# The node stage after the first attention hands over transposed pairs four and three at a time, and sums over node types with two additions

## The chip, the cores and the metric

The kernel runs on one core of a Trainium2 chip. The metric is the device time of that core in microseconds (us). The engines have short names: PE is TensorE (PEld is its weight load), DVE is VectorE, ACT is ScalarE, POOL is GpSimd, and SP is SyncE, which issues the plain DMAs. The granted clock is the share of TensorE's full clock that the chip gave; 0.50 is its level of 1.2 GHz and 1.00 that of 2.4 GHz.

## The reference, cut to what matters

A graph network with 12,500 nodes of 64 features and 200,000 edges runs four layers, each on the normalised node features, each adding its result to `x`. The change lies in the node stage of the first layer, behind the sums over the edges:

```
k, q, v = typed_linear(x, Wk|Wq|Wv, ntype)            # first phase
alpha   = softmax of the edge scores over each dst     # edge phase
h       = segment_sum(m * alpha, dst)                  # edge phase: numerators and denominators
return typed_linear(h, Wa, ntype)                      # THIS stage: a 64x64 matrix for each of 4 node types

def typed_linear(x, W, types):
    out = 0
    for t in range(4):
        out = out + where(types == t, x @ W[t], 0.0)
    return out
...
x = x + first_layer                                    # THIS stage
h = maximum(_layernorm(x), 0.0)                        # THIS stage: the second layer's input
z = h @ Wa ; gate_proj = h @ Wg ; scores               # THIS stage: the second layer's table of node rows
```

The kernel works out `x @ W[t]` for all four types at once (256 columns), multiplies by a one-hot of the node's type and adds the four parts.

## The kernel before, in words

The phases follow each other with a barrier between: a first phase, the edge phase of the attention, a short carry phase, the node stage of this case (`attention_end_phase`), the edge phase and the node stage of the second layer, and three layers of edge sums. In all the edge phases POOL issues one indirect DMA of 128 rows after another (L864), 7820 in all.

In the node stage 12,544 padded nodes lie as 98 tiles of 128 nodes. They are worked in 7 groups (`GROUPS`) of 14 tiles (`GRP`), so a tensor of a group is 128 x 14 x 64, 896 numbers in each partition. Two tiles lie side by side, 128 features wide, and make a pair; a group has 7 pairs (`HALF`). For group i:

- POOL fetches the group's edge sums with 14 indirect DMAs (L1208); all 98 are issued at the stage's start, in order of the groups. When a group's scores are ready it writes them out with 14 more (L1214).
- DVE `take(i)` waits for the 14 fetches, divides the sums by the denominators and leaves the messages in `msg` (L1236, L1238, L1242).
- PE `out_of_group(i)` turns each pair by a transpose into a PSUM bank `ps_t` (L1324), ACT copies it to `ht` (`copy_turned`, L1288), and PE multiplies it with the four types' matrices (L1340): two products for a pair, on the upper and the lower 64 rows, into two banks `ps_o`. With y counting pairs, the transpose of pair y+1 stands ahead of the products of pair y. There are two `ps_t` banks and two `ht` buffers.
- DVE `give(i)` takes two pairs at once (`TWOS`): it multiplies PSUM with the one-hot into `sel` (L1254, twice for each of the four z), sums the four types (L1259), adds to X (L1261), normalises into H (`norm_cols`, L253 to L268; its square root is on ACT, `norm_root`, L275) and works out the scores `s2` (L1265, L1268).
- PE and ACT `rows_of_group(i)` turn the 7 pairs of H the same way, multiply them with `W1` (L1358) into `ps_r`, and ACT copies three pairs at a time (`THREES`) to `rows` (L1309), which SP stores.

The orders on the engines are written out by hand. DVE runs take(0), then for each i: take(i+1), keep_gate(i-2), give(i). ACT runs for each i: the copies of the messages of group i, `rows_of_group(i-1)`, the square root of group i. PE runs for each i: `out_of_group(i)`, `rows_of_group(i-1)`. So the square root that DVE needs in the middle of give(i) stands on ACT behind all of the rows of group i-1. `s_mm` counts finished message pairs, `s_hmm` finished rows pairs, `s_tr` transposes and `s_ht` copies.

Of the kernel before, what the change touches and what calls it, by code (L numbers as in the profile page):

```python
# [27 lines left out]
P = 128  # L28
N = 12500
E = 200000  # L30
D = 64
# [1130 lines left out]
def attention_end_phase(nc, ctx, g, agg):  # L1162
# [3 lines left out]
    s_sel, s_upd = map(sem, ("selected", "updates"))  # L1166
# [21 lines left out]
    assert len(TWOS) % 2 == 0  # L1188

    def turn_of_message(i, y):  # L1190
        return y if i == 0 else HALF + (i - 1) * 2 * HALF + y

    def turn_of_h(i, y):
        return (2 * HALF * (i + 1) if i < GROUPS - 1 else 2 * HALF * GROUPS - HALF) + y

    with ExitStack() as inner:
# [33 lines left out]
        def _(dve):  # L1230
            v = nc.vector
            def take(i):
# [7 lines left out]
                if i >= 2:  # L1240
                    dve.wait_ge(s_tr, turn_of_message(i - 2, HALF - 1) + 1)
# [4 lines left out]
            def give(i):  # L1246
                cols = slice(i * GRP, i * GRP + GRP)
                for z, ys in enumerate(TWOS):
                    dve.wait_ge(s_mm, i * HALF + ys[-1] + 1)
# [9 lines left out]
                v.tensor_reduce(upd, sel.rearrange("p t (k f) -> p t f k", k=NT), AX, ALU.add).then_inc(s_upd, 1)  # L1259
# [25 lines left out]
        def _(act):  # L1285
            def copy_turned(n):
                act.wait_ge(s_tr, n + 1)
                nc.scalar.copy(ht[n % 2], ps_t[n % 2][:, 0:P]).then_inc(s_ht, 1)  # L1288

            def messages_of_group(i):  # L1290
                for y in range(HALF):
                    if y < 2:
                        wait(act, s_hmm, (i - 1) * HALF)
                    wait(act, s_mm, i * HALF + max(y - 1, 0))
                    copy_turned(turn_of_message(i, y))

            def rows_of_group(i):
                for w, ys in enumerate(THREES):
                    for y in ys:
                        if y < 2:  # L1300
                            wait(act, s_mm, min(i + 2, GROUPS) * HALF)
                        wait(act, s_hmm, i * HALF + max(y - 1, 0))
                        copy_turned(turn_of_h(i, y))
                    act.wait_ge(s_hmm, i * HALF + ys[-1] + 1)
# [16 lines left out]
        def _(pe):  # L1321
            def turn(n, pair):
                wait(pe, s_ht, n - 1)
                nc.tensor.transpose(ps_t[n % 2][:, 0:P], pair, g.ident[:, :]).then_inc(s_tr, 1)  # L1324

            def out_of_group(i):
                pe.wait_ge(s_msg, i + 1)
                pair = lambda y: msg[i % 2][:, 2 * y:2 * y + 2, :].rearrange("p t f -> p (t f)")
                turn(turn_of_message(i, 0), pair(0))
                for y in range(HALF):  # L1330
                    n = turn_of_message(i, y)
                    if y + 1 < HALF:
                        turn(n + 1, pair(y + 1))
                    pe.wait_ge(s_ht, n + 1)
                    z, slot = y // 2, y % 2
                    if slot == 0:
                        wait(pe, s_sel, i * len(TWOS) + z - 1)
                    for b in range(2):
                        r = slice(b * D, b * D + D)
                        ins = nc.tensor.matmul(ps_o[b][z % 2][:, slot * NT * D:(slot + 1) * NT * D],  # L1340
                                               ht[n % 2][r, :], g.Wout[r, :], start=True, stop=True)
                    ins.then_inc(s_mm, 1)

            def rows_of_group(i):
                pe.wait_ge(s_n, (i + 1) * NORM_OPS)
                pair = lambda y: g.H[:, i * GRP + 2 * y:i * GRP + 2 * y + 2, :].rearrange("p t f -> p (t f)")
                turn(turn_of_h(i, 0), pair(0))
                for w, ys in enumerate(THREES):
                    for slot, y in enumerate(ys):
                        n = turn_of_h(i, y)  # L1350
                        if y + 1 < HALF:
                            turn(n + 1, pair(y + 1))
                        pe.wait_ge(s_ht, n + 1)
# [959 lines left out]
```

## Time and profile before

| | us |
|---|---|
| median of 3 runs | 13276.4 (13261.65 to 13276.62) |
| profiled execution, device time | 13250.5 |
| its span | 13248.7 |
| the node stage in it: first fetch (L1208) to the start of the last score DMA (L1214) | 2700.2 to 3022.8 |
| first work of the next phase | 3035.9 |

The stage is 323 us of 13,249, 2.4%. The profile counts an engine as busy while an instruction runs. PE's ends are modelled: its rows tell when an instruction was handed to the array and how long it should take, and who waits for its result shows when that was there. The bracket in a row of the timeline is the engine's idle time before it and what ended it; "remote" there means that the profile knows no instruction whose end fits, and "issue" that no wait is seen. The profiled execution is 26 us shorter than the median of the three runs and 11 us shorter than the shortest.

### The profile page before, as it was taken

What the parts mean: (1) busy time and instruction counts of PE and PEld (TensorE: products, weight loads), DVE (VectorE), ACT (ScalarE), POOL (GpSimd) and SP (SyncE); (2) the same over time, 40 slices, a digit from 0 to 9 for tenths busy, and PEclk for the clock granted to TensorE, in tenths of its full rate; (3) what the DMA queues carried; (4) which work ended last, traced back from release to release, by engine and by line L of the source; (5) the groups of instructions that cost most, each with busy time, mean ns of one, the idle gap of its engine ahead of it and who ended that gap; (6) DMA issues with size and microseconds to landing.
All of it is one profiled execution on the core that took longest, in us unless ns stands there. A gap on an engine that the chain in (4) does not pass through costs nothing. (4 is left out here: it accounts for less than half of the span.)

```text
span 13248.7 us, 37564 instructions
## 1 busy us (share of the span) xinstructions
PE 1392.0 (11%) x6735; PEld 1006.9 (8%) x6735; DVE 4039.7 (30%) x5465; ACT 3484.7 (26%) x4624; POOL 9102.4 (69%) x8728
## 2 busy tenths in 40 slices
PE   5200000030000000395000000200000000000000
PEld 3100000010000000273000000100000000000000
DVE  2255555544544544695111111011111101111110
ACT  2322322312222222275332222122211212221121
POOL 4677777757777776402777777577777767777776
PEclk8655555555555555697555555555555555555555
DMA  7333333313333333001222222111111111111111
GB/s 283 132 99 95 95 100 96 95 31 89 94 99 95 94 94 87 14 1 31 62 58 61 58 58 58 42 50 46 49 46 46 48 39 50 46 49 46 46 48 42
DMA packets 404824, 919.06 MB, mean 69 GB/s; under 512 B 171046, under 2 KB 195277, under 8 KB 389496
## 3 DMA queue, kind: packets, MB, share of 16 engines
q0 software_dynamic: 278944, 386.91, 13.3%
q1 hardware_dynamic: 121832, 529.42, 10.9%
q14 instruction: 176, 1.44, 0.0%
q10 hardware_dynamic: 3824, 0.50, 0.0%
q8 instruction: 48, 0.79, 0.0%
HBM read 456.45 MB, written 459.77 MB: 69 GB/s over the span
## 5 line engine op out<-in xcount | busy, mean ns | idle before, releaser
L864 POOL DMA_INDIRECT arena<-tab,src x6256 | 6544.2, 1046 | 2893.7 <-issue 2103.0
L2235 DVE TENSOR_TENSOR_SCAN arena<-cv_keep,arena 128x768 f32<-128x768 f32 (+1 forms) x476 | 752.0, 1627 | 5754.5 <-issue 4533.5
L864 POOL DMA_INDIRECT arena<-tab,spread x1564 | 1651.7, 1056 | 510.2 <-issue 510.2
L2097 ACT COPY arena<-arena 128x1472 f32<-128x1472 f32 x204 | 545.3, 2673 | 3002.8 <-DMA arena<-tab,src 3002.8
L2102 ACT COPY arena<-arena 128x1472 f32<-128x1472 f32 (+1 forms) x204 | 588.4, 2884 | 552.4 <-DVE arena L2235 463.2
L1089 PE MATMUL e_t<-ident,arena 128*68 128x128 f32 (+1 forms) x2 | 0.8, 394 | 4426.1 <-PEq L1424 2216.7
L2159 PE MATMUL cv_t<-ident,arena 128*81 128x128 f32 (+1 forms) x294 | 138.0, 469 | 2912.8 <-ACT arena L2109 1671.9
L2096 ACT COPY arena<-arena 128x368 f32<-128x368 f32 x68 | 55.3, 813 | 1351.3 <-issue 1322.7
L2173 PE MATMUL cv_t<-ident,arena 128*64 128x128 f32 (+1 forms) x3 | 1.3, 425 | 3391.4 <-ACT arena L2102 3391.4
L951 ACT ACTIVATE ae_prob<-arena 128x92 f32<-128x92 f32 x68 | 17.1, 251 | 1228.4 <-issue 942.8
L1874 DVE TENSOR_SCALAR arena<-arena 128x448 bf16<-128x448 f16 x1252 | 325.2, 329 | 43.2 <-issue 21.1
L1493 DVE TENSOR_TENSOR arena<-arena,ge_small 128x23 f32<-128x23 f32 x68 | 13.3, 195 | 1065.3 <-DMA arena<-tab,src 1065.3
L1089 PEld LDWEIGHTS e_t<-ident,arena 128*68 128x68 f32 (+1 forms) x2 | 0.3, 131 | 4426.4 <-issue 4426.4
L1757 PE MATMUL po_u<-arena,Hn 128*128 128x448 bf16 x1564 | 301.4, 355 | 289.7 <-DVE Hn L1864 289.7
L1025 DVE TENSOR_TENSOR arena<-arena,ae_prob 128x1472 f32<-128x1472 f32 x68 | 260.1, 3825 | 219.6 <-issue 215.5
L1456 ACT ACTIVATE ge_decay<-arena 128x768 f32<-128x768 f32 x68 | 56.4, 830 | 1015.0 <-issue 902.1
L992 DVE TENSOR_TENSOR_SCAN ae_work<-ae_keep,arena 128x768 f32<-128x768 f32 x136 | 240.1, 1765 | 221.8 <-remote 146.6
L1757 PE MATMUL po_u<-arena 128*128 128x448 bf16 x1564 | 298.8, 352 | 0.2 <-DVE arena L1874 0.2
L943 ACT ACTIVATE ae_work<-arena 128x768 f32<-128x768 f32 x136 | 208.4, 1533 | 300.8 <-issue 261.0
L2159 PEld LDWEIGHTS cv_t<-ident,arena 128*81 128x81 f32 (+1 forms) x294 | 53.9, 183 | 2949.7 <-ACT arena L2109 1683.0
L1034 DVE TENSOR_TENSOR_SCAN arena<-ae_work,arena 128x768 f32<-128x768 f32 x136 | 238.8, 1756 | 115.2 <-issue 101.7
L1497 DVE TENSOR_TENSOR arena<-arena,ge_small 128x1472 f32<-128x1472 f32 x68 | 258.7, 3804 | 0.2 <-issue 0.2
(369 smaller groups left out, 7017.6 us busy)
## 6 DMA issues: line engine op xcount, KB each, us to landing
rows<-arena SPq DMA_DIRECT2D x68, 1506.5 KB
arena<-tab,src POOLq DMA_INDIRECT x6256
rows3b<-arena SPq DMA_DIRECT2D x136, 736.0 KB
rows<-arena SPq DMA_DIRECT2D x68, 920.0 KB
rows<-arena SPq DMA_DIRECT2D x68, 828.0 KB
tab<-arena SPq DMA_DIRECT2D x49, 1024.0 KB
q_start<-arena SPq DMA_DIRECT2D x32, 1564.0 KB
arena<-q_start SPq DMA_DIRECT2D x68, 736.0 KB
```

Of the source, the lines that this page charges most:

```text
L864: pool.indirect_dma_start(out=rows[b][:, j, :], out_offset=None, in_=table, in_offset=bass.IndirectOffsetOnAxis(ap=idx[:, at:at + 1].bitca ...
L943: return nc.scalar.activation(works.rearrange("p (h d) j -> p h d j", h=HH), args[:, 0, :, h0:h0 + HH].rearrange("p j h -> p h j").unsquee ...
L992: v.tensor_tensor_scan(out=work[:, :], data0=keep[:, :], data1=qts[:, x * HF * C1:(x + 1) * HF * C1], initial=0.0, op0=ALU.mult, op1=ALU.a ...
L1025: v.tensor_tensor(mix[:, :, 1:C1].rearrange("p (h d) j -> p j h d", h=H), kv[:, :, D:2 * D].rearrange("p j (h d) -> p j h d", h=H), prob.u ...
L1034: ins = v.tensor_tensor_scan(out=part, data0=work[:, :], data1=part, initial=0.0, op0=ALU.mult, op1=ALU.add)
L1497: v.tensor_tensor(peak[:, :, 1:C1].rearrange("p f j -> p j f"), r[:, :, D:2 * D], pre.unsqueeze(2).to_broadcast([P, C, D]), ALU.mult).then ...
L1757: ins = nc.tensor.matmul(ps_u[:, x, 0:half], wide[c % 2][:, x * P:x * P + P, j], ring[:, n % RING, :], start=(n == 0), stop=(n == J - 1))
L1874: v.tensor_scalar(ring[:, n % RING, :], iota_hi, hi[:, n:n + 1], None, ALU.is_equal).then_inc(s_hot, 1)
L2097: nc.scalar.copy(chain[:, 0:D, 1:C1], rin[b].rearrange("p j f -> p f j")).then_inc(s_in, 1)
L2102: nc.scalar.copy(rows.rearrange("p j f -> p f j"), chain[:, :, 1:C1]).then_inc(s_copied, 1)
L2159: nc.tensor.transpose(ps_t[b][0:K_Z, 0:P], hd[b][:, 0:K_Z], g.ident[:, :]).then_inc(s_tr, 1)
L2235: ins = v.tensor_tensor_scan(out=part, data0=keep[:, 0:(f1 - f0) * C1], data1=part, initial=0.0, op0=ALU.mult, op1=ALU.add)
```

## The change

Turned pairs are handed over in batches. The messages of a group go as four pairs and three (`FOURS`), the rows as three, three and one (`THREES`): PE writes a batch of transposes side by side into one bank and signals once, ACT copies the whole bank part with one instruction into an `ht` buffer four times as wide, and PE then multiplies the batch. `s_mm` is now counted once per two pairs, and `s_hmm` once per batch. Both batches of messages are turned before the first product. On ACT the next batch of rows is copied before the products of the present one are copied out. On DVE the sum over types becomes an addition of the left 128 columns of `sel` to the right 128 (in place), and one of the left 64 to the next 64. The bytes, the products and the fetches are the same.

```diff
-        ht[b], at = view(g, at, P)
+        ht[b], at = view(g, at, 4, P)
...
+    FOURS = [range(y, min(y + 4, HALF)) for y in range(0, HALF, 4)]
...
-                v.tensor_reduce(upd, sel.rearrange("p t (k f) -> p t f k", k=NT), AX, ALU.add).then_inc(s_upd, 1)
+                v.tensor_tensor(sel[:, :, 0:2 * D], sel[:, :, 0:2 * D], sel[:, :, 2 * D:4 * D], ALU.add).then_inc(s_half, 1)
+                dve.wait_ge(s_half, i + 1)
+                v.tensor_tensor(upd, sel[:, :, 0:D], sel[:, :, D:2 * D], ALU.add).then_inc(s_upd, 1)
...
-            def copy_turned(n):
+            def copy_turned(n, count):
                 act.wait_ge(s_tr, n + 1)
-                nc.scalar.copy(ht[n % 2], ps_t[n % 2][:, 0:P]).then_inc(s_ht, 1)
+                nc.scalar.copy(ht[n % 2][:, 0:count, :].rearrange("p t f -> p (t f)"), ps_t[n % 2][:, 0:count * P])\
+                  .then_inc(s_ht, 1)
 
             def messages_of_group(i):
-                for y in range(HALF):
-                    if y < 2:
-                        wait(act, s_hmm, (i - 1) * HALF)
-                    wait(act, s_mm, i * HALF + max(y - 1, 0))
-                    copy_turned(turn_of_message(i, y))
+                for u, ys in enumerate(FOURS):
+                    wait(act, s_hmm, (i - 1) * len(THREES))
+                    wait(act, s_mm, i * len(TWOS))
+                    copy_turned(turn_of_message(i, u), len(ys))
+
+            def turned_rows(i, w):
+                if w < 2:
+                    wait(act, s_mm, min(i + 2, GROUPS) * len(TWOS))
+                wait(act, s_hmm, i * len(THREES) + max(w - 1, 0))
+                copy_turned(turn_of_h(i, w), len(THREES[w]))
...
             def out_of_group(i):
                 pe.wait_ge(s_msg, i + 1)
                 pair = lambda y: msg[i % 2][:, 2 * y:2 * y + 2, :].rearrange("p t f -> p (t f)")
-                turn(turn_of_message(i, 0), pair(0))
-                for y in range(HALF):
-                    n = turn_of_message(i, y)
-                    if y + 1 < HALF:
-                        turn(n + 1, pair(y + 1))
+                for u, ys in enumerate(FOURS):
+                    turn(turn_of_message(i, u), pair, ys)
+                for u, ys in enumerate(FOURS):
+                    n = turn_of_message(i, u)
                     pe.wait_ge(s_ht, n + 1)
```

On PE, at the start of the stage (group 0's messages; `ao_t0` and `ao_t1` are the two banks of transposes, `ao_o..` the banks of products), these rows stood before:

```order
L1324 MATMUL ao_t0<-ident,arena 128x128
L1324 MATMUL ao_t1<-ident,arena 128x128
L1340 MATMUL ao_o00<-Wout,arena 128x256
L1340 MATMUL ao_o10<-Wout,arena 128x256
L1324 MATMUL ao_t0<-ident,arena 128x128
L1340 MATMUL ao_o00<-Wout,arena 128x256
L1340 MATMUL ao_o10<-Wout,arena 128x256
L1324 MATMUL ao_t1<-ident,arena 128x128
```

And at the same place in the changed kernel:

```order
L1332 MATMUL ao_t0<-ident,arena 128x128 x4
L1332 MATMUL ao_t1<-ident,arena 128x128 x3
L1349 MATMUL ao_o00<-Wout,arena 128x256
L1349 MATMUL ao_o10<-Wout,arena 128x256
L1349 MATMUL ao_o00<-Wout,arena 128x256
L1349 MATMUL ao_o10<-Wout,arena 128x256
L1349 MATMUL ao_o01<-Wout,arena 128x256
L1349 MATMUL ao_o11<-Wout,arena 128x256
```

The seven transposes stood between the products one by one and now stand ahead of them; the number of both is unchanged.

On ACT, between two square roots in the middle of the stage (message copies, then those of the rows of the group before), these rows stood before:

```order
L275 ACTIVATE arena<-arena 128x14
L1288 COPY arena<-ao_t 128x128 x10
L1309 COPY arena<-ao_r 128x3x132 x2
L1288 COPY arena<-ao_t 128x128 x3
L1309 COPY arena<-ao_r 128x3x132 x2
L1288 COPY arena<-ao_t 128x128
L1309 COPY arena<-ao_r 128x132 x2
```

And now:

```order
L275 ACTIVATE arena<-arena 128x14
L1291 COPY arena<-ao_t 128x512
L1291 COPY arena<-ao_t 128x384 x3
L1316 COPY arena<-ao_r 128x3x132 x2
L1291 COPY arena<-ao_t 128x128
L1316 COPY arena<-ao_r 128x3x132 x2
L1316 COPY arena<-ao_r 128x132 x2
```

Fourteen copies of turned pairs became five; the square root still stands behind the rows.

On DVE, in give(i), the reduction before:

```order
L1254 TENSOR_TENSOR arena<-ao_o,types 128x2x256 x6
L1254 TENSOR_TENSOR arena<-ao_o,types 128x256 x2
L1259 TENSOR_REDUCE arena<-arena 128x896
L1261 TENSOR_TENSOR X<-X,arena 128x896
L253 TENSOR_SCALAR arena<-X 128x896
```

And now, with the same instructions around it:

```order
L1255 TENSOR_TENSOR arena<-ao_o,types 128x2x256 x6
L1255 TENSOR_TENSOR arena<-ao_o,types 128x256 x2
L1260 TENSOR_TENSOR arena<-arena 128x14x128
L1262 TENSOR_TENSOR arena<-arena 128x896
L1264 TENSOR_TENSOR X<-X,arena 128x896
```

One reduction over 3584 numbers became additions of 1792 and 896.

## Rows read from the trace of the kernel before

**Rows 1.** The page: busy time, share of the span and instructions of each engine.

```profile
PE 1392.0 (11%) x6735; PEld 1006.9 (8%) x6735; DVE 4039.7 (30%) x5465; ACT 3484.7 (26%) x4624; POOL 9102.4 (69%) x8728
```

**Rows 2.** Busy time by window: length, each engine, granted clock, DMA share, GB/s.

```profile
2720.00:2857.00 137.00, 22.76 (x72) 9.79 (x72) 27.58 (x32) 5.13 (x18) 93.03 (x96) 0.50 0.13 22
...
2871.00:3003.00 132.00, 89.42 (x348) 46.39 (x348) 110.39 (x121) 28.18 (x106) 72.48 (x70) 0.53 0.19 31
```

**Rows 3.** Timeline of group 1's messages: start, length, instruction, idle time before.

```profile
2798.70 0.47 PE L1324 MATMUL ao_t<-ident,arena 128*128 128x128 f32 x1
...
2810.52 0.27 ACT L1288 COPY arena<-ao_t 128x128 f32<-128x128 f32 x1 [13.03 <-remote]
2810.84 0.51 PEld L1340 LDWEIGHTS ao_o<-Wout,arena 64*128 64x128 f32 x4 [11.96 <-issue]
...
2824.52 0.27 ACT L1288 COPY arena<-ao_t 128x128 f32<-128x128 f32 x1 [13.73 <-remote]
...
2835.67 1.29 DVE L1254 TENSOR_TENSOR arena<-ao_o,types 128x512 f32<-128x512 f32 x2 [26.70 <-issue]
```

**Rows 4.** Timeline of DVE alone, give(3), take(5) and the start of give(4).

```profile
2902.72 2.48 DVE L1254 TENSOR_TENSOR arena<-ao_o,types 128x512 f32<-128x512 f32 x4
2906.98 1.95 DVE L1254 TENSOR_TENSOR arena<-ao_o,types 128x512 f32<-128x512 f32 x4 [1.79 <-PE ao_o L1340]
2908.96 6.30 DVE L1259 TENSOR_REDUCE arena<-arena 128x896 f32<-128x3584 f32 x1
2915.30 1.15 DVE L1261 TENSOR_TENSOR X<-X,arena 128x896 f32<-128x896 f32 x1
...
2921.66 0.17 DVE L264 TENSOR_SCALAR arena<-arena 128x14 f32<-128x14 f32 x1
2923.61 0.24 DVE L266 RECIPROCAL arena<-arena 128x14 f32<-128x14 f32 x1 [1.77 <-ACT arena L275]
...
2928.98 2.47 DVE L1254 TENSOR_TENSOR arena<-ao_o,types 128x512 f32<-128x512 f32 x4
```

**Rows 5.** Timeline of ACT alone in that cycle: messages of 3, rows of 2.

```profile
2897.23 0.48 ACT L1288 COPY arena<-ao_t 128x128 f32<-128x128 f32 x2
2899.27 0.27 ACT L1288 COPY arena<-ao_t 128x128 f32<-128x128 f32 x1 [1.56 <-PE ao_t L1324]
...
2912.55 0.88 ACT L1309 COPY arena<-ao_r 128x396 f32<-128x396 f32 x2 [2.35 <-PE ao_r L1358]
...
2921.06 0.88 ACT L1309 COPY arena<-ao_r 128x396 f32<-128x396 f32 x2 [3.96 <-remote]
...
2923.35 0.23 ACT L275 ACTIVATE arena<-arena 128x14 f32<-128x14 f32 x1
```

**Rows 6.** Timeline of PE alone in the same cycle.

```profile
2904.15 1.23 PE L1340 MATMUL ao_o<-Wout,arena 64*128 64x256 f32 x4 [0.29 <-DVE arena L1254]
...
2905.71 2.08 PE L1340 MATMUL ao_o<-Wout,arena 64*128 64x256 f32 x8
2907.72 0.69 PE L1324 MATMUL ao_t<-ident,Hn 128*128 128x128 f32 x2
...
2910.91 0.81 PE L1358 MATMUL ao_r<-W,arena 64*128 64x132 f32 x4
```

**Rows 7.** Groups by line and form, 2873 to 3010 us: busy, mean ns, idle before.

```profile
L1214 POOL DMA_INDIRECT s_start<-small,start_i x73 | 75.4, 1033 | 92.2 <-DVE small L1268 71.8 <-issue 20.4
...
L1259 DVE TENSOR_REDUCE arena<-arena 128x896 f32<-128x3584 f32 x5 | 31.4, 6290 | 0.2
...
L255 DVE TENSOR_REDUCE arena<-arena 128x14 f32<-128x896 f32 x5 | 5.4, 1086 | 0.2
...
L266 DVE RECIPROCAL arena<-arena 128x14 f32<-128x14 f32 x5 | 1.2, 241 | 8.9 <-ACT arena L275 8.9
```

**Rows 8.** Groups of other stages, by line and form, for forms that this stage lacks.

```profile
L1025 DVE TENSOR_TENSOR arena<-arena,ae_prob 128x1472 f32<-128x1472 f32 x68 | 260.1, 3825 | 219.6 <-issue 215.5 <-ACT ae_prob L951 4.1
L759 DVE TENSOR_TENSOR arena<-Hn,types 128x2048 f32<-128x2048 f32 x3 | 6.9, 2292 | 20.2 <-remote 20.1
```

**Rows 9.** Groups of ACT in the first phase, by line and form.

```profile
L540 ACT COPY arena<-fp_tab 128x512 f32<-128x512 f32 x196 | 100.9, 603 | 151.7 <-DMA tab<-arena 63.0 <-remote 47.2 <-PE fp_tab L623 38.8
```

More of the change, by code:

```diff
@@ L1187, in attention_end_phase, with turn_of_message, turn_of_h @@
     THREES = [range(y, min(y + 3, HALF)) for y in range(0, HALF, 3)]
[L1188 to L1194, printed above, removed]
+    FOURS = [range(y, min(y + 4, HALF)) for y in range(0, HALF, 4)]
+    assert len(TWOS) == 2 * len(FOURS) == 4 and len(THREES) == 3
+    def turn_of_message(i, u):
+        return u if i == 0 else 2 + (i - 1) * 5 + u
+    def turn_of_h(i, w):
+        return (5 * i + 4 if i < GROUPS - 1 else 5 * GROUPS - 3) + w
     with ExitStack() as inner:
@@ L1321, in _, with turn @@
         def _(pe):
-            def turn(n, pair):
+            def turn(n, pair, ys):
                 wait(pe, s_ht, n - 1)
-                nc.tensor.transpose(ps_t[n % 2][:, 0:P], pair, g.ident[:, :]).then_inc(s_tr, 1)
+                for slot, y in enumerate(ys):
+                    ins = nc.tensor.transpose(ps_t[n % 2][:, slot * P:slot * P + P], pair(y), g.ident[:, :])
+                ins.then_inc(s_tr, 1)
             def out_of_group(i):
@@ L1328, in out_of_group @@
                 pair = lambda y: msg[i % 2][:, 2 * y:2 * y + 2, :].rearrange("p t f -> p (t f)")
-                turn(turn_of_message(i, 0), pair(0))
-                for y in range(HALF):
-                    n = turn_of_message(i, y)
-                    if y + 1 < HALF:
-                        turn(n + 1, pair(y + 1))
-                    pe.wait_ge(s_ht, n + 1)
[L1335 to L1342, printed above, removed]
+                for u, ys in enumerate(FOURS):
+                    turn(turn_of_message(i, u), pair, ys)
+                for u, ys in enumerate(FOURS):
+                    n = turn_of_message(i, u)
+                    pe.wait_ge(s_ht, n + 1)
+                    for y in ys:
+                        z, slot = y // 2, y % 2
+                        if slot == 0:
+                            wait(pe, s_sel, i * len(TWOS) + z - 1)
+                        for b in range(2):
+                            r = slice(b * D, b * D + D)
+                            ins = nc.tensor.matmul(ps_o[b][z % 2][:, slot * NT * D:(slot + 1) * NT * D],
+                                                   ht[n % 2][r, y - ys[0], :], g.Wout[r, :], start=True, stop=True)
+                        if y in [two[-1] for two in TWOS]:
+                            ins.then_inc(s_mm, 1)
             def rows_of_group(i):
```

33 lines of the change are left out of this document (15 added, 18 removed).

## The prediction, made before the changed kernel ran

> **What bounds the kernel now.** I read the page first. POOL is busy for 69% of the span and DVE for 30% [rows 1], but these are shares over stages with other limits; the change touches 323 us of 13,249, so only that stage counts. Nothing in it can give more than its own 323 us, and every us saved ahead of its last scores is a whole us, since the next phase waits behind a barrier.
>
> The table by windows splits it in two [rows 2]. From 2720 to 2857 us DVE is busy for 27.6 of 137 us: two groups pass there. From 2871 to 3003 us it is busy for 110.4 of 132 us, and five groups pass. The second part is bound by DVE and what DVE waits for. POOL's scores are no bound there: it sits idle for 71.8 us waiting for DVE, and 14 DMAs at about 1.3 us are 18 us of a cycle of 26 [rows 7].
>
> Now one cycle of the second part on DVE [rows 4]. From one give to the next it takes 2928.98 - 2902.72 = 26.3 us. Two stretches are waits: 1.79 us for PE's third z, and 1.77 us in front of L266 for the square root. The largest instruction is the reduction L1259; 6.34 us go by from its start to that of L1261. Over the five cycles the waits ahead of L266 are 8.9 us, of which 0.3 each would stay in any order (the root's own time) [rows 7].
>
> Why is the root late? On ACT it stands behind the rows of the group before, and these end right ahead of it, at 2923.35 [rows 5]. So ACT is already later than DVE by 1.5 us. This is the first thing to see: 3 us taken from DVE alone would only lengthen the wait ahead of L266. The handing over has to shorten ACT's chain too, and the change does both.
>
> The first part is strange [rows 3]. PE was handed a transpose at 2798.70 that should take 0.47 us, and ACT, which waits for it, copies at 2810.52; the copies follow at 2824.52 and so on, 14.0 us apart, where a step of the same kind, with its transpose, takes 1.56 us later (2904.15 to 2905.71 [rows 6]). The granted clock is 0.50 in that stretch and 0.53 in the later one [rows 2], so it doesn't explain a factor of nine. In the later part too PE's results are sometimes late: the third step of L1358 was handed over at 2910.91 and should end at 2911.72, ACT starts at 2912.55; and the next three are waited for 3.96 us by no instruction whose end fits [rows 5, 6]. I don't know the cause, and this is the largest uncertainty.
>
> **The change, part by part.**
>
> *The sum over types.* An addition or reduction over contiguous numbers costs 1.086 us for 896 [rows 7] and 2.292 us for 2048 [rows 8], 1.05 ns a number. So 1792 numbers cost about 2.02 us and 896 cost 1.09; with a gap of 0.03 behind each that is 3.17 against 6.34, a gain of 3.2 us in each group. The other bound is a DVE form that costs 2.6 ns a number, L1025 at 3.825 us for 1472 [rows 8]: 4.7 + 2.3 = 7.0 us, a loss of 0.7. L1025 writes with a stride of 24 numbers; the new additions read and write runs of 128 and 64, like L1261 with its 1.15 us [rows 4], so I take 3.2.
>
> The Trainium skill (VectorE: DVE Perf Modes, the perf-mode tier table) has tensor_reduce and fp32 tensor_tensor both at one result a cycle. By that rule alone 3584 numbers would cost some 3.9 us by the price of 1.05 ns, and the additions would gain only 0.7 us a group. The row says 6.29 us for the reduction [rows 7], 1.75 ns a number, against 1.21 for L255 with its contiguous 64. The page SBUF — State Buffer (its note on cachelines) says that accesses which cross to a new 16-byte line each time pay; L1259 reads its four types 64 numbers apart, so the trace agrees with that, and the row decides.
>
> *The third z.* It waits for the sixth pair's products. Before, the two L1340 steps after DVE's first z each stood behind a transpose and a copy: handed over at 2904.15 and 2905.71, 1.56 us apart. Back to back a step costs 2.08 - 1.23 = 0.85 us [rows 6]. The sixth pair comes 0.7 us earlier, so the wait of 1.79 becomes 1.1. Five groups: 3.5 us. The copy ahead of the first product grows from 0.27 to about 0.60 us [rows 9], but the products of the first pairs are wanted only 5.5 us after the root [rows 4], and four take 3.8: hidden. If that cover were gone it would cost 0.3 us a group.
>
> *The rows on ACT.* Count from DVE's first z, T. Before, the root came at T + 20.6 (2923.35 - 2902.72). After: the first z ends at T + 1.3, the last three message steps end 3 us later (two at 0.85 and one of 1.23), three transposes take 0.9 (0.69 for two, 0.2 for one more), their copy 0.5. A batch of three steps L1358 takes 0.81 and two more at about 0.5, an estimate between 0.4 and 0.81: 1.8 us, and two copies L1309 take 0.88 [rows 5, 6]. Twice that is 5.4, the last pair 1.3, semaphores some 0.5. The root could come at T + 12.9. DVE would want it at T + (2921.83 - 2902.72) - 3.2 - 0.7 = T + 15.2. If all goes well the waits ahead of L266 vanish: 8.9 - 5 x 0.3 = 7.4 us. If PE's results stay as late as now (0.8 and 3.1 us in this cycle), the root comes at T + 16.8 and the wait is what it was. I take half, 3.7 us.
>
> *The first part.* Group 1 ends with its own reduction, on the path: 3.2 us. Group 0's reduction lies inside the strange stretch; if that ends at a time of its own, its gain is lost. I take 1.5 of 3.2.
>
> *The sum:* 1.5 + 3.2 + 5 x 3.2 + 3.5 + 3.7 = 28 us. Against the profiled execution that is 13250.5 - 28 = 13222.5, or 0.21%; that execution lies 26 us below the median, so on the median it is 13276 - 28 = **13248 us**. The store of the rows and the 14 score DMAs behind the last group stay.
>
> **The rivals.**
> *PE becomes the bound.* A cycle holds 14 steps and 14 transposes. ACT's longer wait for a batch of three steps is 3.96 us [rows 5], 1.3 us a step; I estimate 1.4 us for a step when PE is late and a quarter of that for a transpose, which has a quarter of the passes: 17.5 x 1.4 = 24.5 us a cycle. If all of PE's denser work came at this rate, the five cycles would gain 1.8 us each, and with group 1 the sum is 12 us: 13264. For it speaks that lateness follows quick steps; against it, that steps 1.56 us apart in the messages are on time.
>
> *The late results belong to each hand-over.* In group 1 ACT's copies come 13 to 14 us apart [rows 3]. If a hand-over itself costs that, two in place of seven would save 5 x 13 = 65 us beside the rest, 13185 us. Against it: a constant 14.0 us is what PE's queue would give if its work ran slowly, and the work is the same.
>
> *Slower.* Same place as the first rival: it decides where the late rate is above 26.3 / 17.5 = 1.5 us a step. At 1.8 us a cycle takes 31.5, five of them 26 us more: 13302. For it speaks the first part, where 14.0 us for a step and its transpose make 11.2 a step. Against it, the 1.3 us a step in the longest wait of the second part.
>
> *The additions save little.* At the reduction's own 1.75 ns a number they take 4.8 us, gain 1.6 a group and leave 17 us: 13259. At 1.05 ns a number for reduction and addition alike, which no row of this reduction bears out, 11 us would be left: 13265. (That is what the tier table of the Trainium skill's page on VectorE comes to.)
>
> *The additions cost more*, at L1025's price: 5 us lost against about 5 us from the hand-overs: 13276, no change. The same time comes out if ACT's chain doesn't shorten and DVE's gain all turns into waits ahead of L266.
>
> **How the numbers follow.** My forecast (20 to 37 us gained) gets 0.54, PE as the bound 0.18, the hand-overs 0.09, slower 0.07, additions that save little 0.04, no change 0.08. A measurement of this kernel tells about 0.2%, 27 us, from no change. The forecast's middle lies just there, so a little over half of it counts as faster: 0.30 + 0.09 = 0.39; same 0.24 + 0.18 + 0.04 + 0.08 = 0.54; slower 0.07. The likeliest case alone is 13239 to 13257. The range leaves out the hand-overs and the slower case; at the low end it takes in the forecast's best case (37 us gained) and 17 us for the runs, whose three already spread by 15 us; at the high end the case of no change: 13222 to 13280.
>
> **What would show it.** Right: L1260 near 2.02 and L1262 near 1.09 us; about 21 to 23 us from give to give in the second part; a wait of about 1.1 us for the third z; ACT with a copy of 512 near 0.60 us. The wait ahead of L266 tells the middle from the first rival: near 0.3 us, or 2 and more. Wrong: a stretch after 2720 that lasts clearly longer or shorter than 137 us, which would outweigh all that I have summed, or an in-place addition above 4 us.

## The result, and the profile after

| | before | after |
|---|---|---|
| median | 13276.4 us (17 runs, 13261.65 to 13279.51) | 13245.5 us (17 runs, 13231.12 to 13249.97) |
| profiled execution | 13250.5 | 13244.2 |

The ratio is 0.9977, with a 95% interval of 0.9971 to 0.9984: 30.9 us or 0.23% faster, 2.5 us below the predicted 13248. The two profiled executions differ by 6.3 us only: in the one of after the stage's first take (L1237) comes 18.2 us later, and 4.4 us more are lost behind the stage, both in phases that the change doesn't touch. So the stage is counted from its first take here:

| from DVE's first take to | before | after |
|---|---|---|
| L266 of group 1 | 152.9 | 150.0 |
| L266 of group 6 | 283.5 | 250.8 |
| start of the last score reduction | 286.0 | 253.3 |
| start of the last score write | 303.9 | 275.0 |
| first work of POOL in the next phase | 317.7 | 288.8 |

All of the stage's gain but 2.9 us comes in the second part. DVE's timeline there, the end of one take and the give behind it, answers to [rows 4]:

```profile
2913.27 4.55 DVE L1255 TENSOR_TENSOR arena<-ao_o,types 128x512 f32<-128x512 f32 x8
2917.85 2.03 DVE L1260 TENSOR_TENSOR arena<-arena 128x1792 f32<-128x1792 f32 x1
2919.91 1.09 DVE L1262 TENSOR_TENSOR arena<-arena 128x896 f32<-128x896 f32 x1
2921.04 1.11 DVE L1264 TENSOR_TENSOR X<-X,arena 128x896 f32<-128x896 f32 x1
...
2927.36 0.20 DVE L264 TENSOR_SCALAR arena<-arena 128x14 f32<-128x14 f32 x1
2927.84 0.24 DVE L266 RECIPROCAL arena<-arena 128x14 f32<-128x14 f32 x1 [0.28 <-ACT arena L275]
...
2933.21 2.48 DVE L1255 TENSOR_TENSOR arena<-ao_o,types 128x512 f32<-128x512 f32 x4
```

Read it from the brackets. Ahead of L266 only the square root's own 0.28 us is left, and in this give the eight products run through without a wait for the third z; in the next it is 1.06 us. From this give to the next it is 19.9 us in place of 26.3; a give with the wait takes 20.9. The wait for the third z goes with the granted clock. Where it is 1.06 us, PE worked at a granted clock of 0.50 at the start of the give (2891 to 2896, 2932 to 2937 and 2971 to 2976 us); where it is 0, at 0.84 and 0.83 (2912 to 2917, 2952 to 2957). Over the second part the clock is 0.62, and it was 0.53 [rows 2]. ACT's timeline of the same cycle shows the other side, against [rows 5]:

```profile
2917.69 0.48 ACT L1291 COPY arena<-ao_t 128x384 f32<-128x384 f32 x1 [8.97 <-PE ao_t L1332]
2918.33 0.48 ACT L1291 COPY arena<-ao_t 128x384 f32<-128x384 f32 x1 [0.16 <-issue]
2919.84 0.88 ACT L1316 COPY arena<-ao_r 128x396 f32<-128x396 f32 x2 [1.03 <-PE ao_r L1367]
...
2921.85 0.88 ACT L1316 COPY arena<-ao_r 128x396 f32<-128x396 f32 x2 [0.96 <-issue]
2923.69 0.44 ACT L1316 COPY arena<-ao_r 128x132 f32<-128x132 f32 x2 [0.96 <-issue]
2927.59 0.21 ACT L275 ACTIVATE arena<-arena 128x14 f32<-128x14 f32 x1 [3.47 <-DVE arena L264]
```

The rows are done at 2924 and ACT waits 3.47 us for L264 of DVE. The roles have changed: DVE's own work is the cycle. Two groups by line (2887 to 2990 us) answer to [rows 7]:

```profile
L1215 POOL DMA_INDIRECT s_start<-small,start_i x66 | 79.2, 1200 | 48.2 <-DVE small L1271 28.7 <-issue 19.5
...
L1260 DVE TENSOR_TENSOR arena<-arena 128x1792 f32<-128x1792 f32 x5 | 10.1, 2025 | 0.2
```

POOL's score writes now fill the whole cycle: 1.20 us on average with 0.30 between, so fourteen take 21 us. The last 84 follow one another without a gap, from 2890.91 to 3012.99 us. From the last score reduction to the last write it is 21.7 us, 17.9 before: 3.8 us of the 32.7 that DVE gained are given back in POOL's queue. Some writes are longer beside the new additions, as this one:

```profile
2958.68 2.02 DVE L1260 TENSOR_TENSOR arena<-arena 128x1792 f32<-128x1792 f32 x1
2959.09 2.47 POOL L1215 DMA_INDIRECT s_start<-small,start_i  x1 [0.30 <-issue]
```

In each of five cycles one write lies across L1260 and L1262 and takes 1.82 to 2.47 us. Before, 25 writes lay beside the reduction L1259, and every one took 0.97 us.

The first part, DVE's timeline:

```profile
2767.98 1.29 DVE L1255 TENSOR_TENSOR arena<-ao_o,types 128x512 f32<-128x512 f32 x2 [10.00 <-remote]
2790.38 1.29 DVE L1255 TENSOR_TENSOR arena<-ao_o,types 128x512 f32<-128x512 f32 x2 [21.11 <-remote]
...
2843.61 1.29 DVE L1255 TENSOR_TENSOR arena<-ao_o,types 128x512 f32<-128x512 f32 x2 [25.95 <-remote]
2866.01 1.29 DVE L1255 TENSOR_TENSOR arena<-ao_o,types 128x512 f32<-128x512 f32 x2 [21.11 <-remote]
2875.11 1.95 DVE L1255 TENSOR_TENSOR arena<-ao_o,types 128x512 f32<-128x512 f32 x4 [7.82 <-remote]
```

Two pairs take 22.4 us (2767.98 to 2790.38, 2843.61 to 2866.01), 11.2 us for the two products of a pair, the same as the step that the forecast worked out from [rows 3]. The last late result is used 138.1 us after the first take, before it was 137.8. Fewer hand-overs change nothing in that stretch.

### The profile page after: what moved, and what is told of

Same layout as the page of the kernel before. It is cut to its first block and busy times, and to the rows that moved or that the text cites. A ratio compares the mean times of both kernels' runs of the same rounds, so it can differ in the third digit from the quotient of the medians.

```text
span 13242.4 us, 37433 instructions
## 1 busy us (share of the span) xinstructions
PE 1352.0 (10%) x6735; PEld 1005.3 (8%) x6735; DVE 4015.6 (30%) x5472; ACT 3476.7 (26%) x4561; POOL 9106.3 (69%) x8728
## 5 line engine op out<-in xcount | busy, mean ns | idle before, releaser
L1883 DVE TENSOR_SCALAR arena<-arena 128x448 bf16<-128x448 f16 x1252 | 324.8, 330 | 37.4 <-PE po_u L1766 20.4
```

Of the source, the lines that this page charges most:

```text
L1883: v.tensor_scalar(ring[:, n % RING, :], iota_hi, hi[:, n:n + 1], None, ALU.is_equal).then_inc(s_hot, 1)
```

## The experiments

Twelve kernels ran, in four sets, each on a chip of its own. Each set ran the kernel before too, and its medians there are 13278.1 (additions, hand-overs, takes behind the fetches, PE at work before), 13280.4 (messages, rows, loads by SP, take 1 behind the fetches), 13281.3 (give(0) ahead, loads by POOL) and 13263.8 us (the two with held writes). So times of different sets are compared by their ratio to before. "Stage" is from DVE's first take to the start of the last score reduction, in the profiled execution (before 286.0, after 253.3).

| kernel | median | ratio to before, 95% | stage | L266 of 1 to L266 of 6 |
|---|---|---|---|---|
| additions alone | 13256.1 | 0.9982, 0.9973 to 0.9991 | 265.6 | 113.2 |
| hand-overs alone | 13268.4 | 0.9991, 0.9982 to 1.0 | 276.7 | 121.0 |
| additions and messages | 13248.4 | 0.9976, 0.9966 to 0.9985 | 253.7 | 101.2 |
| additions and rows | 13253.5 | 0.9980, 0.9971 to 0.9989 | 263.5 | 111.0 |
| (the whole change) | 13245.5 | 0.9977, 0.9971 to 0.9984 | 253.3 | 100.8 |

The last column is 130.7 before.

### The two halves: additions alone, hand-overs alone

Additions alone, in the kernel before:

```diff
-                v.tensor_reduce(upd, sel.rearrange("p t (k f) -> p t f k", k=NT), AX, ALU.add).then_inc(s_upd, 1)
+                v.tensor_tensor(sel[:, :, 0:2 * D], sel[:, :, 0:2 * D], sel[:, :, 2 * D:4 * D], ALU.add).then_inc(s_half, 1)
+                dve.wait_ge(s_half, i + 1)
+                v.tensor_tensor(upd, sel[:, :, 0:D], sel[:, :, D:2 * D], ALU.add).then_inc(s_upd, 1)
```

> The kernel before with the two contiguous additions in place of the one strided reduction; every hand-over from TensorE to ScalarE stays a pair. The additions are 3.17 us shorter per group. Theory A (the forecast's reading of rows 4 and 5: between two give() VectorE waits for ScalarE's square root, and that comes by ScalarE's and TensorE's own chain of eight pairs of messages and eight pairs of rows): in the steady groups the time saved turns into a longer wait ahead of L266 (8.9 us becomes about 12), the cycle stays 26.1 us, and only the first groups keep something: 0 to 5 us faster, 13271 to 13276. Theory B (VectorE's own work ends the cycle, so each of seven groups gives back its 3.2 us): 22 us faster, 13254. Between them: the square root is asked for by VectorE's L266 only after the additions, and ScalarE takes it between two of its pairs, so a part of 3.2 us may come through.

Hand-overs alone is the same edit the other way round in the changed kernel.

> The changed kernel with the one strided reduction put back (6.29 us per group in place of 3.1): the hand-overs alone. Theory A (in the changed kernel VectorE's own work of 20.2 us per group is the cycle, ScalarE and TensorE have slack): the cycle becomes 20.2 + 3.2 = 23.4 us, five of them and the rest about 22 us slower than the changed kernel at most, so 9 to 16 us faster than before: 13260 to 13267. Waits ahead of L266 stay near 0.3 us. Theory B (the hand-overs bring nothing by themselves, since ScalarE's chain was not the bound): within 3 us of before, and the additions alone bring all of the 31 us. With the additions-alone run: if the two runs' gains add to clearly less than 31 us, the two parts of the change need each other.

Measured: 22.0 us faster for the additions (stage 20.4), 9.7 for the hand-overs (stage 9.3). The interval of the hand-overs reaches 1.0, so their gain rests on the stage. Theory A of the first run falls, and with it a sentence of the forecast: taking 3.2 us from DVE alone was to lengthen the wait ahead of L266. DVE's timeline with the additions alone:

```profile
2913.79 2.48 DVE L1254 TENSOR_TENSOR arena<-ao_o,types 128x512 f32<-128x512 f32 x4
2918.04 1.95 DVE L1254 TENSOR_TENSOR arena<-ao_o,types 128x512 f32<-128x512 f32 x4 [1.78 <-PE ao_o L1342]
2920.03 2.04 DVE L1259 TENSOR_TENSOR arena<-arena 128x1792 f32<-128x1792 f32 x1
...
2931.40 0.24 DVE L266 RECIPROCAL arena<-arena 128x14 f32<-128x14 f32 x1 [1.65 <-ACT arena L275]
```

The wait is 1.65 us, against 1.77 in [rows 4]. The root came at T + 17.35 (2931.14 on ACT, T = 2913.79), before at T + 20.6: it came earlier by the same 3.3 us. ACT's timeline shows where:

```profile
2923.75 0.88 ACT L1311 COPY arena<-ao_r 128x396 f32<-128x396 f32 x2 [2.49 <-PE ao_r L1360]
...
2928.86 0.88 ACT L1311 COPY arena<-ao_r 128x396 f32<-128x396 f32 x2 [1.86 <-PE ao_r L1360]
...
3004.08 0.88 ACT L1311 COPY arena<-ao_r 128x396 f32<-128x396 f32 x2 [1.58 <-PE ao_r L1360]
...
3008.34 0.88 ACT L1311 COPY arena<-ao_r 128x396 f32<-128x396 f32 x2 [1.58 <-PE ao_r L1360]
```

Between the two batches of rows lie 5.1 us, 8.5 in [rows 5] (2912.55 to 2921.06), and 4.26 for the last group, behind which no messages stand. So of ACT's chain before 4.3 us a cycle were PE's late results, and 3.4 of them went with the strided reduction. Batches of rows 8.6 to 6.4 us apart are also what the kernel with the reduction and the new hand-overs has, in five of its seven groups; the changed kernel has 2.0 to 2.8.

The reduction alone doesn't make the rows late, though. In the kernel before, the rows of group 0 pass beside the reduction of group 1, while POOL issues nothing (from 2842 to 2876 us):

```profile
2858.66 6.30 DVE L1259 TENSOR_REDUCE arena<-arena 128x896 f32<-128x3584 f32 x1
...
2860.29 0.88 ACT L1309 COPY arena<-ao_r 128x396 f32<-128x396 f32 x2 [1.58 <-PE ao_r L1358]
...
2864.55 0.88 ACT L1309 COPY arena<-ao_r 128x396 f32<-128x396 f32 x2 [1.58 <-PE ao_r L1358]
```

The batches are 4.26 us apart, at a granted clock of 0.50, as they are for the last group, where POOL writes and no reduction runs. With the hand-overs alone these two groups have 2.75 us. So in both kernels with the reduction the rows are late by some us just where the reduction and POOL's indirect writes run together. How the two make them late is not shown, and no run changes the writes alone in this part.

With the hand-overs alone the cycle is 26.3 us in two of five groups and 23.1 to 23.7 in two others (L266 at 2893.63, 2919.97, 2946.24, 2969.95, 2993.02); its waits ahead of L266 are 2.66 and 2.60 us in the first two and short after. The theory's 23.4 us in every cycle missed by that, and 13268.4 us lies just above its range. The gains of the halves add to 31.7 us of time and 29.7 of stage, where both together have 30.9 and 32.7: nearly additive, though the intervals of the times are some 12 us wide to either side.

### Which hand-over: messages or rows

Additions, messages four and three, rows one pair at a time:

```diff
             def rows_of_group(i):
-                turned_rows(i, 0)
                 for w, ys in enumerate(THREES):
-                    if w + 1 < len(THREES):
-                        turned_rows(i, w + 1)
+                    for y in ys:
+                        if y < 2:
+                            wait(act, s_mm, min(i + 2, GROUPS) * len(TWOS))
+                        wait(act, s_hmm, i * HALF + max(y - 1, 0))
+                        copy_turned(turn_of_h(i, y), 1)
```

> Additions, and the messages handed over in four and three; the rows of H stay at one pair per hand-over. With the additions alone a steady group takes 22.98 us, of which VectorE waits 1.78 us ahead of the third z step and 1.65 us (0.28 of it the square root itself) ahead of L266. Theory A (the wait of the third z step belongs to the messages, the wait ahead of L266 to the rows, as the forecast had it): 1.78 becomes 1.07 or less and 1.65 stays, a cycle of about 22.3 us, some 4 us faster than the additions alone, 13252. Theory B (both waits end one chain on ScalarE that runs through messages and rows together, so that any part of it made shorter moves both): both waits shrink, the one ahead of L266 to about 1 us or 0.28, the cycle 20.9 to 21.5 us, 13246 to 13250.

Additions, rows three, three and one, messages one pair at a time:

```diff
             def messages_of_group(i):
-                for u, ys in enumerate(FOURS):
-                    wait(act, s_hmm, (i - 1) * len(THREES))
-                    wait(act, s_mm, i * len(TWOS))
-                    copy_turned(turn_of_message(i, u), len(ys))
+                for y in range(HALF):
+                    if y < 2:
+                        wait(act, s_hmm, (i - 1) * len(THREES))
+                    wait(act, s_mm, i * HALF + max(y - 1, 0))
+                    copy_turned(turn_of_message(i, y), 1)
```

> Additions, and the rows of H handed over in three, three and one; the messages stay at one pair per hand-over. Theory A (each wait has its own cause): the wait ahead of L266 falls from 1.65 to 0.28 us, the third z wait stays at 1.78, a cycle of 21.6 us, about 7 us faster than the additions alone, 13249. Theory B (one chain): both waits fall, 20.9 us or less per group, 13245 to 13247. If neither wait moves, the rows were never what ScalarE's square root came behind.

DVE with the messages in batches:

```profile
2942.16 1.95 DVE L1255 TENSOR_TENSOR arena<-ao_o,types 128x512 f32<-128x512 f32 x4 [1.04 <-PE ao_o L1345]
...
2954.14 0.24 DVE L266 RECIPROCAL arena<-arena 128x14 f32<-128x14 f32 x1 [0.28 <-ACT arena L275]
```

And with the rows in batches:

```profile
2925.93 1.95 DVE L1255 TENSOR_TENSOR arena<-ao_o,types 128x512 f32<-128x512 f32 x4 [1.78 <-PE ao_o L1350]
...
2939.26 0.24 DVE L266 RECIPROCAL arena<-arena 128x14 f32<-128x14 f32 x1 [1.59 <-ACT arena L275]
```

The messages take away most of both waits: 1.04 in place of 1.78 and 0.28 in place of 1.65, a cycle of 20.6 to 20.9 us in four of five, and 12.0 of the stage's 12.3 us. On ACT the first batch of rows comes 7.8 us behind DVE's first z in place of 10.0, and the second 4.25 us behind the first in place of 5.1. The rows in batches move neither wait in the first two cycles (22.9 and 23.0 us); in the third and fourth the wait ahead of L266 falls to 0.78 and 0.28 us (22.2 and 21.7 us). They bring 2.1 us. Theory B of the first run holds and neither theory of the second does: the root stands behind the rows on ACT, but its time moves with the messages ahead of them. The seven single copies of rows could nearly have stayed. One rival stays open: over the second part the granted clock is 0.53 with the additions alone, 0.59 with the rows in batches and 0.69 with the messages, and no run tells apart what the batches bring and what the clock brings. The 4.25 us between the batches of rows need no higher clock: the kernel before has 4.26 at 0.50.

### The late stretch: does it belong to PE's start or to POOL's fetches?

The changed kernel, all takes behind all fetches:

```diff
             def take(i):
                 cols = slice(i * GRP, i * GRP + GRP)
+                for k in range(GROUPS if i == 0 else 0):
+                    dve.wait_ge(s_end[k], 16 * GRP)
```

> The changed kernel, but VectorE's first take waits until the fetches of all seven groups have landed, some 85 us later than now. It asks what the stretch belongs to in which TensorE's results come late (one step of a pair of pairs 22.4 us, until 138 us after the first take, in both kernels). Theory A (it belongs to the fetches that GpSimd issues meanwhile): with the fetches over, groups 0 and 1 run like the others, from the first take to L266 of group 1 about 50 us in place of 150, and the run is 0 to 20 us shorter than the changed kernel's 13245. Theory B (it belongs to TensorE's own start after a long rest): the stretch moves along, 150 us from the first take to L266 of group 1, and the run is about 85 us longer, near 13330.

PE at work ahead of the stage:

```diff
+        @block.tensor
+        def _(pe):
+            for c in range(NC - 8, NC):
+                pe.wait_ge(s_rows, c)
+                for n in range(12):
+                    nc.tensor.transpose(early[:, n % 4 * P:n % 4 * P + P], g.ident[:, :], g.ident[:, :])
```

> The changed kernel with work for TensorE added ahead of the stage: in the last eight chunks of the edge phase (31.5 us each, TensorE without any work there) twelve transposes of the identity per chunk into a PSUM tensor that nobody reads. The transposes wait for nobody's results and nobody waits for them; late ones of 2.8 us each would need 34 us per chunk, a little more than a chunk has. Theory A (the late results belong to the first 138 us or so of TensorE's work after a long rest, or to its first 60 to 100 instructions): the late stretch is spent before the stage begins, groups 0 and 1 run at the pace of the others, 50 in place of 150 us, and the run is up to 90 us shorter: 13155 to 13200. Theory B (they belong to the fetches, or to the profile alone): the stage is as it was, 13240 to 13255.

Plain loads in place of the fetches, by SP:

```diff
+                for t in range(i * GRP, i * GRP + GRP):
+                    sp.dma_start(agg[:, t, :], g.rows0[t * P:t * P + P, :]).then_inc(s_end[i], 16)
```

> The changed kernel with the stage's 98 indirect fetches that GpSimd issues replaced by 98 plain loads of as many bytes from SyncE's queue (neighbouring rows in place of the wanted ones, so the aggregates are other numbers). Theory A (the late results go with GpSimd's issuing of indirect fetches): no result comes late, groups 0 and 1 take about 50 us from the first take in place of 150, and the loads themselves may come faster, so the run is 80 to 120 us shorter: 13125 to 13165. Theory B (they go with bytes landing in SBUF meanwhile, whoever issued them): the late stretch is as long as the loads take plus some 30 us, and only their faster or slower landing shows.

And by POOL (the same line on its queue):

> The changed kernel with the 98 indirect fetches of the stage replaced by 98 plain loads of as many bytes that GpSimd issues from its own queue (neighbouring rows in place of the wanted ones, so the aggregates are other numbers). The same loads from SyncE's queue left no late result: 44.7 us from the first take to L266 of group 1. Theory A (late results belong to the indirect fetches themselves): as with SyncE's loads, 45 to 55 us, and a run of 13130 to 13150. Theory B (they belong to GpSimd's issuing of any transfer while TensorE works): results come late as in the changed kernel for as long as GpSimd issues; with loads that take it about 1 us each, L266 of group 1 100 to 150 us after the first take, and a run of 13190 to 13245.

| kernel | first take to L266 of group 1 | time |
|---|---|---|
| changed kernel | 150.0 | 13245.5 |
| takes behind the fetches | 47.9 | 13251.5 (one run) |
| PE at work before | 148.6 | 13247.1 (ratio 0.9977, 0.9967 to 0.9986) |
| loads by SP | 44.7 | 13134.6 (one run) |
| loads by POOL | 45.5 | 13151.8 (one run) |

With the takes behind the fetches the first product of the stage comes 12.5 us after the take and the next on time:

```profile
2845.66 0.19 DVE L1239 TENSOR_SCALAR arena<-arena 128x56 f32<-128x56 f32 x1 [127.65 <-DMA arena<-rows,end_i]
...
2858.19 2.48 DVE L1257 TENSOR_TENSOR arena<-ao_o,types 128x512 f32<-128x512 f32 x4 [8.71 <-remote]
2861.74 1.95 DVE L1257 TENSOR_TENSOR arena<-ao_o,types 128x512 f32<-128x512 f32 x4 [1.07 <-PE ao_o L1351]
```

The two kernels with plain loads take other rows than the wanted ones, so they tell of time only. POOL issues its 98 plain loads from 2724 to 2776 us, which covers the products of groups 0 and 1. So the stretch is not PE's start (it comes with work ahead, and with plain loads it is gone, though PE starts as it did), nor bytes that land in SBUF (SP's loads), nor POOL's issuing (its plain loads); it goes with POOL's indirect fetches. Waiting them out costs about what it saves: the 0 to 20 us that were expected of it didn't come.

### Where the stretch ends, and whether it can be cut

Take 1 behind all fetches, first with give(0) behind it in the order as it stood, then with give(0) ahead:

```diff
+                for k in range(GROUPS if i == 1 else 0):
+                    dve.wait_ge(s_end[k], 16 * GRP)
```

> The changed kernel, but VectorE's second take (group 1) waits until the fetches of all seven groups have landed; group 0 is taken and given as now, during the fetches. With every take behind the fetches the late results were gone (47.9 us from the first take to L266 of group 1 in place of 150) and the run stayed near 13251. Theory A (the results of TensorE come late only while fetches are issued and as long after them as work was heaped up meanwhile; group 0's seven pairs at 11.2 us a pair fit into the 123 us of the fetches): group 0 is done by the end of the fetches and group 1 starts at once at the full pace, so one group's 20 us are saved against the variant with all takes behind, L266 of group 1 some 28 us after the last landing: 13226 to 13238, better than both kernels. Theory B (the lateness has a length of its own once it has begun, about 138 us): L266 of group 1 comes near 2905 us, 10 to 20 us slower than the changed kernel, 13255 to 13265.

```diff
             take(0)
-            for i in range(GROUPS):
+            give(0)
+            take(1)
+            for i in range(1, GROUPS):
```

> The changed kernel with VectorE's work in another order: take 0, give 0, and only then take 1, which waits until the fetches of all seven groups have landed (in the run before this one give 0 stood behind the waiting take 1, so nothing of group 0 could be given during the fetches). Theory A (results of TensorE come late while GpSimd's fetches are issued, and afterwards only by what was heaped up meanwhile): group 0 is done near 2812 us as in the changed kernel, nothing is heaped up, and group 1 starts at the last landing near 2845 at full pace; the variant with all takes behind the fetches needed 28.0 us from its first take to its first L266, so L266 of group 1 near 2875 in place of 2887: 10 to 14 us faster than the changed kernel, 13230 to 13237. Theory B (once begun, the lateness lasts some 138 us whatever is asked of TensorE): group 1's results are late until about 2875 too, L266 of group 1 at 2890 to 2900, no gain or a loss, 13245 to 13258.

The first: 13246.8 (0.9974, 0.9964 to 0.9984), no different from the changed kernel and in neither theory's range: on DVE give(0) itself stands behind the waiting take, so nothing of group 0 could be given during the fetches. But its timeline has the last late result of the stage already 117.0 us behind the first take (2739.79), 13.0 us after the last fetch, and POOL wrote nothing between:

```profile
2856.80 0.76 DVE L1257 TENSOR_TENSOR arena<-ao_o,types 128x256 f32<-128x256 f32 x2 [4.61 <-remote]
```

The second: 13250.0 (0.9976, 0.9967 to 0.9986). Its timeline of DVE speaks against theory A, since group 1's results are late though the fetches have landed:

```profile
2851.32 0.19 DVE L1239 TENSOR_SCALAR arena<-arena 128x56 f32<-128x56 f32 x1 [30.39 <-DMA arena<-rows,end_i]
...
2870.37 1.29 DVE L1257 TENSOR_TENSOR arena<-ao_o,types 128x512 f32<-128x512 f32 x2 [15.23 <-remote]
2880.87 3.37 DVE L1257 TENSOR_TENSOR arena<-ao_o,types 128x512 f32<-128x512 f32 x6 [9.22 <-remote]
```

2880.87 is again 138.0 us behind the first take. But here, as in the changed kernel, group 0's fourteen score writes follow the last fetch without a gap, and with the takes behind the fetches they didn't. That gave a third theory, and one line:

```diff
+            pool.wait_ge(s_mm, 2 * len(TWOS))
             for i in range(GROUPS):
                 pool.wait_ge(s_s2, i + 1)
```

> The changed kernel with one wait more on GpSimd: after the 98 fetches its score writes (14 indirect writes per group) begin only once all products of group 1 are there. In the changed kernel group 0's fourteen writes follow the last fetch without a gap, 2843 to 2861 us, and TensorE's results stay late until 2875; with all takes behind the fetches no write stood behind the fetches, and the results were on time some 12 us after the last landing. Theory A (results are late as long as GpSimd's string of indirect transfers has no gap, and some 12 us after it): the last late result comes near 2857 in place of 2875, L266 of group 1 near 2870 in place of 2887, and the stage and the run are 10 to 17 us shorter, 13228 to 13236, if the writes moved back don't end the stage (seven groups by about 19 us from 2858 end at 2991 to 2996; the last group's scores come near 2975 and its writes take 18). Theory B (lateness lasts 138 us from the first take, as in eight of the runs so far): nothing moves until 2875, no gain, or a loss of the 15 us by which the writes start later: 13245 to 13262.

> Both: take 0, give 0, then take 1 once all fetches have landed, and GpSimd's score writes held until the products of group 1 are there. Theory A (a string of indirect transfers without a gap makes the results late; with its end at the last fetch nothing is late when group 1 starts): from take 1 at about 2846 us (on the changed kernel's clock) 28 us to L266 of group 1 as in the run with all takes behind the fetches, so 2874 in place of 2887: 8 to 13 us faster than the changed kernel, 13232 to 13238. Theory B (138 us from the first take): group 1's results are late until 2875 as before, L266 of group 1 at 2888 or later, 13247 to 13262.

POOL and DVE with the writes held:

```profile
2847.77 0.95 POOL L1209 DMA_INDIRECT arena<-rows,end_i  x1 [0.30 <-issue]
2859.74 1.00 POOL L1216 DMA_INDIRECT s_start<-small,start_i  x1 [11.02 <-PE ao_o L1350]
```

```profile
2856.88 1.29 DVE L1256 TENSOR_TENSOR arena<-ao_o,types 128x512 f32<-128x512 f32 x2 [15.51 <-remote]
2859.05 1.95 DVE L1256 TENSOR_TENSOR arena<-ao_o,types 128x512 f32<-128x512 f32 x4 [0.88 <-remote]
...
2871.06 0.24 DVE L266 RECIPROCAL arena<-arena 128x14 f32<-128x14 f32 x1 [0.28 <-ACT arena L275]
```

The last late result comes at 116.0 us behind the first take (2740.85) in place of 138, 8 us after POOL's fetches end; theory B falls, as it did with the 117.0 us of take 1 behind the fetches. L266 of group 1 comes at 130.2 in place of 150.0 (with both edits 118.2 and 133.7 us), the last score reduction at 233.5 in place of 253.3. But the last score write starts 26.8 us later still, at 260.3: of 19.8 us gained, 5.1 go to POOL's queue. The median is 13228.6, ratio 0.9970 (0.9958 to 0.9982); with both edits 13223.7, 0.9968 (0.9956 to 0.9980), last write at 265.0. Both intervals overlap the changed kernel's. The stage of the profiled execution is 14.7 us (held) and 10.0 us (both) shorter up to the last write; that the whole kernel is faster than the changed one is likely and not shown.

## Why the prediction was right, and where its reasons weren't

*The sum over types* was priced at 2.02 + 1.09 us; measured 2.025 and 1.09. It pays in six of the seven groups. The perf-mode tier table of the Trainium skill (VectorE: DVE Perf Modes), by which, as the forecast estimated, reduction and additions would differ by 0.7 us a group, is not borne out: the rows say 6.29 us against 3.12, and 22.0 us came, not some 5. One sentence of the reasoning was wrong: "3 us taken from DVE alone would only lengthen the wait ahead of L266" is refuted by the additions alone (22.0 us). It took ACT's chain up to the root as fixed at T + 20.6 us when only DVE changes; 3.4 us of that chain were late results that went with the reduction, so the root came at T + 17.35. Seven tenths of the gain are this one edit.

*The third z.* Forecast 1.1 us, 3.5 us in all; measured 1.06, 0, 1.06, 0 and 1.07, so 1.79 x 5 - 3.2 = 5.8 us. The forecast's 1.1 is right at the granted clock of the rows it was read from (0.50 from 2903 to 2912 us); the two zeros come at 0.83 and 0.84, and a rise of the clock was no term of the sum.

*The wait ahead of L266.* Forecast 3.7 of 7.4 us, measured all: the term was half of what came. Its place was wrong too. It was put down to fewer hand-overs of the rows; the runs show that they bring 2 us of the stage and those of the messages 12 (with a higher clock, as said).

*The first part.* Group 1's 3.2 us came (2.9). Of group 0's 3.2, 1.5 was counted; it is 0, since the late stretch ends 138 us behind the first take in either kernel.

*What stays behind the last group* was taken as unchanged; POOL's queue took 3.8 us. Sum: 0 + 2.9 + 15.9 + 5.8 + 7.5 = 32.1, where the stage has 32.7; these less 3.8 are the 28.9 at the next phase's first work. The forecast's 28 is a term too large, two too small and one missed. That it came within 3 us is in part luck: 6.1 us too little in the two waits stands against 1.5 too much for group 0 and the 3.8 of POOL's queue.

*The rivals.* PE did not become the bound: the cycle is 20.2 us on average (100.8 / 5) where it was to be 24.5. Late results are not a price per hand-over: 11.2 us for a pair's products in both kernels. The additions neither saved little nor cost more.

## What to carry to other kernels

A wait at the end of a chain on another engine doesn't mean that the chain has a length of its own. Here 3.4 us of ACT's chain went together with DVE's reduction, so the time taken from DVE came through in full, and the run of that half alone showed it. Of the hand-overs, those that a cycle starts from (here the messages) were worth 12 us and those right ahead of the wait 2. And when a cycle gets shorter, price the queues that had slack in it: fourteen indirect writes of 1.2 us on average filled the new cycle of 20 us.

## What the runs showed of the hardware

- While POOL issues its 98 indirect fetches, PE's results reach those who wait for them 11.2 us apart for the two products of a pair, and 14.0 us apart with a transpose, though PE's own rows show them handed over long before; on time, products are 0.85 us apart. The granted clock is 0.50 to 0.57 there. Plain loads of as many bytes by SP or POOL don't do it. In all twelve kernels with the indirect fetches, before and after included, the last late result comes 8 to 15 us after the end of the fetches, or of the fourteen indirect writes where these follow the fetches without a gap. Indirect writes by themselves don't do it: the changed kernel's last 84 run without a gap, and DVE waits for PE 1.07 us at most beside them. The mechanism stays open, and so does whether it is there in an execution that nobody records.
- The strided reduction takes 1.75 ns a number. Where it runs together with POOL's indirect writes, the rows of PE come late, in batches 6.4 to 8.6 us apart; with the additions in its place they are 2.0 to 5.1 apart, and beside the reduction with no writes 4.26 (before) and 2.75 (hand-overs alone). Not explained.
- POOL's indirect writes take 1.03 us on average in both kernels with the reduction and 1.10 to 1.15 us in those with the additions (2885 to 3020 us). Beside the reduction every one takes 0.96 or 0.97 us; the one that lies across the two additions takes 1.6 to 2.6 us.
- In the changed kernel the granted clock is 0.62 over the second part, in the kernel before 0.53.
